# Expert tiles of 256 rows, four to a unit, in nine groups of images instead of six

## The chip, the cores and the metric

The kernel runs on one core of one Trainium2 chip. The metric is the device time of one execution in microseconds (us), lower is better; an execution's time is that of its slowest core, and here there is one.

## The reference

The input is 32 images of 32 x 32 pixels with 128 channels, in fp32. Three layers follow one another, each with a residual:

```python
x = x + window_attention(group_norm(x))      # 8x8 windows, shifted by 4, 8 heads of 16, cosine attention with a bias
t = tokens(x)                                # 1024 tokens to an image
t = t + banded_attention(layer_norm(t))      # windows of 128 tokens, 4 heads of 32, each sees 32 tokens back
t = t + experts(layer_norm(t))

def experts(x):                              # 8 experts, hidden size 256
    probs = softmax(x @ gate_w + gate_b)
    top2_vals, top2_idx = top_k(probs, 2)    # two experts to a token
    for e in range(8):
        h = gelu(x @ W1[e] + b1[e])
        out += weight_of_e[:, None] * (h @ W2[e] + b2[e])
```

The change is in the third layer, whose work depends on the data: each token goes to two of eight experts.

## The kernel before, in words

**Passes.** `hybrid_kernel` runs a software pipeline over images: 36 passes i from -1 to 34 (`PASSES` is 35), each of eight steps t. In pass i the image i+1 is loaded and normalised, image i goes through window attention, the scores of i-1 and i-2 through banded attention (12 steps behind, `LAG`), and image i-3 is gated. Every engine has one hand-written list of instructions in that order, and they meet only at semaphores. In each step TensorE (PE) makes scores, VectorE (DVE) adds bias or mask and takes the row maximum, GpSimd (POOL) subtracts it (`below_max`), ScalarE (ACT) takes the exponential, PE transposes and multiplies by the values.

**Sorting by expert.** In pass d+3 the gate of image d computes for each token its two experts, weights, and places in a sorted buffer in DRAM (`gate_*`, L1453 to L1530). GpSimd then writes the image's rows there with 16 indirect DMAs (`scatter`, L1218; three steps of pass d+3 and the first of the next). Images are taken in groups (`GROUPS`, L32): a group has one sorted buffer `x_sorted` with a region for each of the eight experts. At the last image of a group DVE makes a table (`tile_table`, L1532): the buffer row and the expert of each tile of 512 rows. Since the numbers are known only on the chip, as many tiles are computed as the worst case needs, 2 x images x 1024 / 512 + 7.

**Units.** A tile of 512 rows with its expert's weights (a row of 642 floats on each of 128 partitions: W1, W2, both biases) is a unit, two units a pair. A pair needs: loading (`load_pair`, L455, on SyncE's queue SP; in the tail on ScalarE's), eight transposes (`slots_in`, L814), a copy of 1024 columns (`slots_copy`, L1072), four matmuls of 512 columns (`hidden`, L821), four gelus (`gelu`, L1079), sixteen matmuls of 128 columns in two halves each (`expert_out`, L829), two additions of b2 (`slots_back`, L1572) and two stores into `y_sorted` (`store_pair`, L501). Loads read their row number and expert out of the table with `value_load`.

`plan` (L163) lays pairs into the passes: up to three to a pass, in slots 0, 1, 2, whose rows are transposed in step t = 1, 3, 6 (`stage`, L416). The first pair of a group stands in slot 1 or 2 of the fourth pass after the group's last image. Before it, `load_pair` waits for the table and for all scatters of the group, copies one tile of zeros behind each of the eight experts' rows (L462 to L469), waits until these have landed, and only then loads the first rows. What fits into no pass is left for the tail after the last pass.

**Gathering.** When a group's rows are stored, GpSimd reads them back for each image with 16 indirect DMAs (`gather`, L1227), and DVE weights, adds and stores (`sum_experts`, L1579). Passes take one image, from pass 29 (`TWO_SUMS_FROM`) two; what is left follows in the tail. From pass 32 on GpSimd puts a memset of a scratch tile after every indirect DMA (`apart`, L1239), but not behind the gathers of the last four images (`UNPAUSED`). In the tail DVE has the sum of an image behind every 2.5 pairs (L438 to L441):

```python
for c in range(first_tail_sum, IMAGES):
    at = max([at] + [n + 1 for n, u in enumerate(tail) if pairs[u].group == group_of[c]]) + PAIRS_PER_SUM
    (tail_sums[int(at)] if at < len(tail) else late_sums).append(c)
```

While there are no pairs (`i < first_slots`), PE runs one matmul of the identity by 512 columns in every step, whose result nobody reads (L867).

## Time and profile before

| | us |
|---|---|
| median of 3 runs | 3075.22 |
| the three runs | 3070.97, 3075.22, 3096.71 |
| span of the profiled execution, first to last instruction | 3088.7 |

The span is that of one more execution, under the profiler; what of it lies around the span the profile does not give. It is 13.5 us (0.4%) above the median. Times in the trace count from the start of the span. PE busy is matmul time, PEld the loading of its stationary operand; SPq and ACTq are DMAs issued by SyncE and ScalarE. A pass is recognised on PE by L801 (and L745), which stand in its step 4. The stretches of the rows below run from step 4 of one pass to step 4 of the next, or over several such.

### The profile page before, as it was taken

How to read it: one execution, taken by the hardware profiler on the slowest of the kernel's cores; microseconds unless marked ns; L12 is line 12 of the kernel's file. 1: busy time of each engine (PE TensorE's matmuls, PEld its weight loads, DVE VectorE, ACT ScalarE, POOL GpSimd, SP SyncE). 2: the span in 40 equal slices, each digit the busy share in tenths (PEclk: the TensorE clock that was granted, in tenths of full speed). 3: DMA queues.
4: the chain of work that ended last, by engine and by line, in shares of the span. 5: the costliest groups of instructions: out<-in, count | busy, mean ns of one | idle time of the engine just before them, and what ended most of it. 6: DMA issues, size and time to landing. Idle time of an engine off the chain costs nothing.

```text
span 3088.7 us, 77036 instructions
## 1 busy us (share of the span) xinstructions
PE 2544.2 (82%) x27338; PEld 1794.8 (58%) x27338; DVE 1965.5 (64%) x5091; ACT 1865.7 (60%) x3409; POOL 1914.2 (62%) x2270
## 2 busy tenths in 40 slices
PE   6898889989888899889988988899888887676830
PEld 3565655556666666666666666666665665554520
DVE  4577777777666666777676676767776765522222
ACT  3666656666767677677776677767777654432310
POOL 1335555555444444576666576666667878779986
PEclk9998888888999999899999999999999988788965
DMA  5223333334445454144333343434343434456743
GB/s 208 104 110 117 117 132 150 147 127 138 147 173 182 161 183 161 60 148 123 100 122 117 107 144 122 126 96 127 119 149 111 131 109 135 123 171 203 244 127 91
DMA packets 262427, 421.99 MB, mean 137 GB/s; under 512 B 41740, under 2 KB 141080, under 8 KB 261280
## 3 DMA queue, kind: packets, MB, share of 16 engines
q1 hardware_dynamic: 219232, 327.69, 31.2%
q0 software_dynamic: 32768, 67.17, 7.7%
q10 hardware_dynamic: 10048, 22.19, 2.2%
q8 instruction: 223, 3.65, 0.5%
q14 instruction: 156, 1.28, 0.1%
HBM read 198.26 MB, written 231.22 MB: 139 GB/s over the span
## 4 chain that ended last, share of the span: by engine, by line
PE 48%; POOL 17%; ACT 15%; issue 10%; DVE 7%; DMA 2%; ACTq 1%; SPq 1%; POOLq 0%; DVEq 0%
PE bank_m L834 7%; POOL yg L1233 7%; PE bank_m L827 4%; PE bank_to L761 4%; POOL x_sorted L1223 4%; PE bank_s L801 4%; PE bank_s L807 3%; PE bank_s L716 3%; ACT pt_sb_a L1051 2%; POOL xin L1243 2%; PE bank_to L770 2%; PE bank_s L729 2%; ACT L1178 2%; ACT v_a L1036 2%; PE bank_s L739 2%
## 5 line engine op out<-in xcount | busy, mean ns | idle before, releaser
L1223 POOL DMA_INDIRECT x_sorted<-xn_c,place_i x512 | 534.3, 1044 | 282.1 <-PE bank_s L700 109.2
L1233 POOL DMA_INDIRECT yg<-y_sorted,place_i x512 | 521.4, 1018 | 241.1 <-PE bank_to L783 107.5
L1216 POOL TENSOR_TENSOR s_sb_a<-s_sb_a,mx_a 128x512 f32<-128x512 f32 x256 | 267.8, 1046 | 587.7 <-DVE mx_a L1607 586.9
L1599 DVE TENSOR_TENSOR s_sb_a<-bank_s,bias_a 128x512 f32<-128x512 f32 x256 | 176.6, 690 | 355.3 <-PE bank_s L700 257.7
L827 PE MATMUL bank_m<-xe,wk_e 128*128 128x512 f32 x552 | 280.5, 634 | 37.7 <-ACT hid L1084 27.7
L834 PE MATMUL bank_m<-wk_e,hid 128*128 128x128 f32 x2208 | 283.3, 291 | 0.9 <-ACT hid L1084 0.9
L834 PEld LDWEIGHTS bank_m<-wk_e,hid 128*128 128x128 f32 x2208 | 277.7, 208 | 2.2 <-issue 1.9
L1216 POOL TENSOR_TENSOR s_sb_b<-s_sb_b,mx_b 128x512 f32<-128x512 f32 x256 | 269.7, 1054 | 11.5 <-DVE mx_b L1607 11.5
L761 PE MATMUL bank_to<-k_consts,p_sb_b 128*128 128x128 f32 x1024 | 179.0, 300 | 92.2 <-ACT pt_sb_a L1051 56.1
L1051 ACT ACTIVATE pt_sb_b<-bank_to 128x512 f32<-128x512 f32 x256 | 152.5, 596 | 146.4 <-PE bank_to L761 145.7
L1207 POOL TENSOR_TENSOR km_a<-qk_a,k_consts 128x128 f32<-128x128 f32 x512 | 215.7, 445 | 40.0 <-DVE qk_a L1451 35.4
L1056 ACT ACTIVATE p_sb_a<-s_sb_a 128x512 f32<-128x512 f32 x256 | 160.7, 628 | 122.1 <-POOL s_sb_a L1216 121.6
L1084 ACT ACTIVATE hid<-bank_m,wk_e 128x512 f32<-128x512 f32 x276 | 184.2, 686 | 78.7 <-PE bank_m L827 71.4
L700 PE MATMUL bank_s<-km_a,qk_a 32*64 32x128 f32 x4096 | 123.8, 296 | 112.9 <-POOL km_a L1207 52.3
L1056 ACT ACTIVATE p_sb_b<-s_sb_b 128x512 f32<-128x512 f32 x256 | 161.3, 630 | 72.1 <-POOL s_sb_b L1216 69.9
L827 PEld LDWEIGHTS bank_m<-xe,wk_e 128*128 128x128 f32 x552 | 98.5, 199 | 174.3 <-issue 134.9
L761 PEld LDWEIGHTS bank_to<-k_consts,p_sb_b 128*128 128x128 f32 x1024 | 113.5, 147 | 136.8 <-ACT pt_sb_a L1051 98.6
L761 PE MATMUL bank_to<-k_consts,p_sb_a 128*128 128x128 f32 x1024 | 167.3, 286 | 26.0 <-ACT p_sb_a L1056 25.8
L1068 ACT ACTIVATE sum_inv<-bank_to 128x256 f32<-128x256 f32 (+1 forms) x268 | 99.7, 372 | 139.8 <-PE bank_to L783 120.6
L1602 DVE TENSOR_TENSOR s_sb_b<-bank_s,k_consts 128x512 f32<-128x512 f32 x256 | 174.0, 680 | 13.7 <-ACT p_sb_b L1056 11.8
L1584 DVE TENSOR_TENSOR yg<-yg,weight 128x2048 f32<-128x2048 f32 x32 | 74.8, 2338 | 161.0 <-DMA yg<-y_sorted,place_i 161.0
L1576 DVE TENSOR_TENSOR yo<-bank_m,wk_e 128x512 f32<-128x512 f32 x138 | 94.9, 689 | 126.2 <-PE bank_m L834 106.8
(221 smaller groups left out, 6266.7 us busy)
## 6 DMA issues: line engine op xcount, KB each, us to landing
y_sorted<-t_back SPq DMA_DIRECT2D x192, 512.0 KB, 5.5
y_sorted<-yo SPq DMA_DIRECT2D x170, 256.0 KB
wk_e<-in_w_experts_dram SPq DMA_DIRECT2D x134, 321.0 KB
xs<-x_sorted SPq DMA_DIRECT2D x134, 256.0 KB
t_kept<-t SPq DMA_DIRECT2D x64, 256.0 KB
t_back<-t_kept SPq DMA_DIRECT2D x32, 512.0 KB
xin<-in_x_dram SPq DMA_DIRECT2D x128, 112.0 KB
x_res<-in_x_dram SPq DMA_DIRECT2D x256, 56.0 KB
```

The lines of the kernel that those rows point to most:

```text
L761: last = tr(T[:, P * j:P * j + P], p_sb[w][:, j, :], ident)
L827: mm(banks[:, ch, :], w[:, P * ch:P * ch + P], xe[:, m, :], start=True, stop=True).then_inc(z_ready, 1)
L834: last = mm(banks[:, m, P * j:P * j + P], hid[:, CH * m + ch, P * j:P * j + P], w[:, HID + P * ch:HID + P * ch + P], start=(ch == 0), stop ...
L1051: func(flat(pt_sb[w][:, :, :]), T, ACT.Copy).then_inc(pt_copied[w], 1)
L1056: func(flat(p_sb[w][:, :, :]), flat(s_sb[w][:, :, :]), ACT.Exp, scale=1.0 if w == 0 else float(DB) ** -0.5).then_inc(p_ready[w], 1)
L1084: func(hid[:, CH * m + ch, :], banks[:, ch, :], ACT.Gelu, bias=w[:, B1_AT + ch:B1_AT + ch + 1]).then_inc(gelu_ready, 1)
L1207: op = pool.tensor_tensor(km_a[:, n % 2, h, :], keys, const("pair_mask")[:, h:h + 1].to_broadcast([P, P]), ALU.mult)
L1216: pool.tensor_tensor(s[:, :, :], s[:, :, :], m[:, :, None].to_broadcast(shape), ALU.subtract).then_inc(s_sub[w], 1)
L1223: pool.indirect_dma_start(out=x_sorted[group_of[d] % XSIDES].ap(), out_offset=bass.IndirectOffsetOnAxis(ap=place_i[:, d, n:n + 1], axis=0) ...
L1233: pool.indirect_dma_start(out=yg[:, c % 2, n, :], out_offset=None, in_=y_sorted[side].ap(), in_offset=bass.IndirectOffsetOnAxis(ap=place_i ...
L1599: tt(s_sb[0][:, :, :].rearrange("p (r h) n -> p r (h n)", h=2), scores, bias_a[:, kind, :, :].rearrange("p (r h) n -> p r (h n)", h=2), AL ...
L1602: tt(s_sb[1][:, :, :], scores, const("mask_b")[:, None, :].to_broadcast([P, HB, P]), ALU.add).then_inc(s_added[1], 1)
```

## The change

- A tile has 256 rows (`SLOTS`), and a unit is two tiles (`PART = 2`) that each have their own row number, expert and weights. A unit has 512 rows as before, and its buffers are `ROOM` = 512 columns of rows and two sets of weights. A group's worst case falls from 2 x images x 2 + 7 tiles of 512 rows to 2 x images x 4 + 8 tiles of 256.
- Loads and stores are issued by tile: 8 loads to a pair instead of 4, 4 stores instead of 2. A matmul of `hidden` and a gelu take 256 columns and are twice as many.
- `GROUPS` is (3,4,4,4,4,4,4,3,2). The sorted buffers shrink from 65536 to 36864 rows, so filling `y_sorted` takes 108 DMAs instead of 192, clearing the spare rows of `x_sorted` 6 instead of 12.
- `TWO_SUMS_FROM` is 24.
- To make room, weights and places are kept for 16 images, some small tiles share one buffer, and constants that only the start needs lie in a buffer of the gather.

What `plan` makes of these numbers:

| | before | after |
|---|---|---|
| units, pairs | 170, 88 | 164, 82 |
| pairs in passes, in the tail | 68, 20 | 69, 13 |
| first pass with pairs | 10 | 6 |
| passes where a group's first pair is loaded (slot) | 10, 17, 23 (1), 28 (2), 33 (1), tail | 6, 10, 14, 18, 22, 26, 30 (1), 33 (2), tail |
| stretches from step 4 of pass i with fewer than 3 pairs, first pair to pass 29 | 15, 22, 28 (2.5), 16 (0) | 8 (2), 9 (0), 13, 17, 21, 25, 29 (1) |
| images summed in passes, in the tail | 20, 12 | 23, 9 |
| passes that sum two images | 29 to 32 | 24, 26, 27, 30, 31 |
| tail: after which pair (from 0) the sums stand that come before the last pair | 2, 5, 7, 10, 12, 15, 17 | 2, 5, 7, 10, 12 |

```diff
-GROUPS = (7, 7, 6, 5, 4, 3)
-SLOTS = 512
+GROUPS = (3, 4, 4, 4, 4, 4, 4, 3, 2)
+SLOTS = 256
 SUB = SLOTS // P
+PART = 2
+ROOM = PART * SLOTS
+KEPT = 16
...
-MAX_TILES = TOP * MOST // SLOTS + E - 1
+MAX_TILES = TOP * MOST // SLOTS + E
...
-TWO_SUMS_FROM = 29
+TWO_SUMS_FROM = 24
...
-        tiles = list(range(TOP * size * TOKENS // SLOTS + E - 1))
+        tiles = list(range(0, TOP * size * TOKENS // SLOTS + E, PART))
...
-                row = eng.value_load(tiles[0:1, kth:kth + 1], min_val=0, max_val=BUFFER - SLOTS)
-                expert = eng.value_load(tiles[0:1, MAX_TILES + kth:MAX_TILES + kth + 1], min_val=0, max_val=E - 1)
-                rows = x_sorted[side].ap()[bass.ds(row, SLOTS), :].rearrange("(p j) d -> p (j d)", p=P)
-                eng.dma_start(xs_b[b], rows).then_inc(tile_in[b], 16)
-                weights = w_experts[bass.ds(expert, 1), :, :].rearrange("e p n -> (e p) n")
-                eng.dma_start(wk_b[b], weights).then_inc(tile_in[b], 16)
+                for h in range(PART):
+                    at = kth + h
+                    row = eng.value_load(tiles[0:1, at:at + 1], min_val=0, max_val=BUFFER - SLOTS)
+                    expert = eng.value_load(tiles[0:1, MAX_TILES + at:MAX_TILES + at + 1], min_val=0, max_val=E - 1)
+                    rows = x_sorted[side].ap()[bass.ds(row, SLOTS), :].rearrange("(p j) d -> p (j d)", p=P)
+                    eng.dma_start(xs_b[b][:, SLOTS * h:SLOTS * h + SLOTS], rows).then_inc(tile_in[b], 16)
+                    weights = w_experts[bass.ds(expert, 1), :, :].rearrange("e p n -> (e p) n")
+                    eng.dma_start(wk_b[b][:, h, :], weights).then_inc(tile_in[b], 16)
...
-                pe.wait_ge(tile_in[b], 32 * use)
+                pe.wait_ge(tile_in[b], 32 * PART * use)
...
-                    mm(banks[:, ch, :], w[:, P * ch:P * ch + P], xe[:, m, :], start=True, stop=True).then_inc(z_ready, 1)
+                    for h in range(PART):
+                        own = slice(SLOTS * h, SLOTS * h + SLOTS)
+                        last = mm(banks[:, ch, own], w[:, h, P * ch:P * ch + P], xe[:, m, own], start=True, stop=True)
+                    last.then_inc(z_ready, 1)
...
-                    func(hid[:, CH * m + ch, :], banks[:, ch, :], ACT.Gelu,
-                         bias=w[:, B1_AT + ch:B1_AT + ch + 1]).then_inc(gelu_ready, 1)
+                    for h in range(PART):
+                        own = slice(SLOTS * h, SLOTS * h + SLOTS)
+                        last = func(hid[:, CH * m + ch, own], banks[:, ch, own], ACT.Gelu,
+                                    bias=w[:, h, B1_AT + ch:B1_AT + ch + 1])
+                    last.then_inc(gelu_ready, 1)
```

Two places show how instructions move. First ScalarE in the tail, kernel before: the load of the second unit of a pair (it stands twice in a row, once to a unit; `xs` is the rows, `wk_e` the weights, TENSOR_LOAD and ISA are `value_load` and address arithmetic), then the gelus of the pair before it and the copy of the next.

```order
L476 TENSOR_LOAD table
L476 ISA x2
L477 TENSOR_LOAD table
L477 ISA x2
L479 ISA
L479 DMA xs<-x_sorted 128x512
L481 ISA
L481 DMA wk_e<-in_w_experts_dram 128x642
L1084 ACTIVATE hid<-bank_m,qk_a 128x512 x2
L1084 ACTIVATE hid<-bank_m,wk_e 128x512 x2
L1077 ACTIVATE xe<-bank_s 128x1024
```

The same place after the change:

```order
L482 TENSOR_LOAD table
L482 ISA x2
L483 TENSOR_LOAD table
L483 ISA x2
L485 ISA
L485 DMA xs<-x_sorted 128x256
L487 ISA
L487 DMA wk_e<-in_w_experts_dram 128x642
L1097 ACTIVATE hid<-bank_s,wk_e 128x256 x8
L1088 ACTIVATE xe<-bank_to 128x1024
```

The load now stands four times in a row ahead of the gelus, each with half the rows and the whole weights, and there are eight gelus of half the width.

Second, SyncE in pass 33, kernel before: behind the store of slot 0's pair comes the load of slot 2's.

```order
L513 DMA y_sorted<-yo 128x512
L476 TENSOR_LOAD table
L476 ISA x2
L477 TENSOR_LOAD table
L477 ISA x2
L479 ISA
L479 DMA xs<-x_sorted 128x512
```

After the change, the same place (the store is the last of four):

```order
L520 DMA y_sorted<-yo 128x256
L469 TENSOR_LOAD table
L469 ISA x2
L472 ISA
L472 DMA x_sorted<-x_sorted 16x2048
L469 TENSOR_LOAD table
```

The eight copies of zeros of a new group now stand here between the store and the load; in the kernel before, pass 33 has them in slot 1, ahead of this store.

## Rows read from the trace of the kernel before

**Rows 1.** Chain of waits, from 2734.1 to the end: its summary line.

```profile
by line: POOL yg L1233 41.1%; issue 15.6%; POOL xin L1243 13.8%; DMA qk_a<-in_w_experts_dram 3.6%; DMA wk_e<-in_w_experts_dram 3.3%; POOL x_sorted L1223 3.0%; PE bank_m L827 1.8%; PE bank_s L834 1.5%; DMA yg<-y_sorted,place_i 1.5%; DVE yg L
```

**Rows 2.** Timeline, DVE: start, length, line, form, count, idle before and releaser.

```profile
2793.31 2.29 DVE L1584 TENSOR_TENSOR yg<-yg,weight 128x2048 f32<-128x2048 f32 x1 [20.97 <-DMA yg<-y_sorted,place_i]
...
2993.66 2.29 DVE L1584 TENSOR_TENSOR yg<-yg,weight 128x2048 f32<-128x2048 f32 x1 [15.90 <-DMA yg<-y_sorted,place_i]
...
3078.93 2.29 DVE L1584 TENSOR_TENSOR yg<-yg,weight 128x2048 f32<-128x2048 f32 x1 [16.17 <-DMA yg<-y_sorted,place_i]
```

**Rows 3.** GpSimd by line, 2765 to 3062.5: duration min/median/max in ns.

```profile
L1233 POOL DMA_INDIRECT yg<-y_sorted,place_i x180: 940/951/2736, 2765.8 to 3061.4; - x180
L1243 POOL MEMSET xin<- x129: 538/539/551, 2765.1 to 2992.1; 128x512 f32 x129
```

**Rows 4.** Windows: length, busy PE PEld DVE ACT POOL (instructions), PE clock, DMA share, GB/s.

```profile
751.10:1175.70 424.60, 381.26 (x4326) 276.27 (x4327) 271.40 (x765) 305.53 (x546) 193.44 (x240) 0.96 0.48 167
1328.90:1761.20 432.30, 388.81 (x4326) 282.17 (x4326) 295.66 (x780) 305.73 (x546) 274.03 (x321) 0.94 0.38 117
1839.90:2264.00 424.10, 380.23 (x4319) 276.03 (x4319) 298.81 (x794) 304.64 (x545) 272.88 (x319) 0.96 0.38 115
1255.00:1328.90 73.90, 62.29 (x741) 43.14 (x739) 59.81 (x162) 47.21 (x94) 54.10 (x64) 0.89 0.36 108
1175.70:1255.00 79.30, 69.15 (x826) 51.70 (x826) 53.56 (x152) 55.41 (x103) 37.44 (x46) 0.93 0.39 138
...
2346.10:2438.40 92.30, 79.47 (x874) 57.30 (x869) 67.81 (x159) 61.41 (x110) 77.32 (x80) 0.93 0.42 126
2438.40:2535.90 97.50, 82.05 (x851) 58.39 (x847) 64.70 (x146) 60.24 (x106) 77.53 (x80) 0.88 0.39 119
2535.90:2625.70 89.80, 65.15 (x655) 48.00 (x654) 55.37 (x143) 43.52 (x79) 77.59 (x89) 0.89 0.40 122
2625.70:2706.20 80.50, 55.98 (x406) 41.40 (x405) 42.74 (x98) 34.60 (x64) 57.29 (x71) 0.77 0.41 126
...
2734.10:3088.70 354.60, 171.76 (x921) 118.36 (x921) 86.89 (x96) 71.02 (x96) 296.56 (x355) 0.75 0.55 169
```

**Rows 5.** Windows, steps 4 of passes 6 to 30 in one.

```profile
461.90:2438.40 1976.50, 1763.94 (x20039) 1265.17 (x20038) 1389.46 (x3737) 1376.71 (x2511) 1186.87 (x1395) 0.94 0.41 134
```

**Rows 6.** Timeline, SP and PE, first pair of a group in pass 17.

```profile
1300.49 9.75 SPq L468 DMA_DIRECT2D x_sorted<-x_sorted  x8
1314.38 0.37 SPq L479 DMA_DIRECT2D xs<-x_sorted  x1
...
1317.16 0.33 SPq L481 DMA_DIRECT2D wk_e<-in_w_experts_dram  x1
...
1321.40 0.66 PE L818 MATMUL bank_m<-k_consts,xs 128*128 128x128 f32 x4 [0.56 <-DMA wk_e<-in_w_experts_dram]
```

**Rows 7.** Timeline, pass 33: DVE and PE around slot 2.

```profile
2698.59 0.68 DVE L1576 TENSOR_TENSOR yo<-bank_m,wk_e 128x512 f32<-128x512 f32 x1
...
2712.51 1.06 PE L818 MATMUL bank_m<-k_consts,xs 128*128 128x128 f32 x8 [1.07 <-DVE yo L1576]
```

**Rows 8.** ScalarE by line and form: count, busy us, mean ns, idle before.

```profile
L1084 ACT ACTIVATE hid<-bank_m,wk_e 128x512 f32<-128x512 f32 x276 | 184.2, 686 | 78.7 <-PE bank_m L827 71.4
...
L1051 ACT ACTIVATE pt_sb_b<-bank_to 128x512 f32<-128x512 f32 x256 | 152.5, 596 | 146.4 <-PE bank_to L761 145.7
...
L1068 ACT ACTIVATE sum_inv<-bank_to 128x256 f32<-128x256 f32 x244 | 93.4, 383 | 137.6 <-PE bank_to L783 120.6 <-PE bank_to L773 12.7 <-issue 1.1
```

**Rows 9.** Timeline, ScalarE in the tail: a pair's loads, and the new group's.

```profile
2759.31 0.34 ACTq L479 DMA_DIRECT2D qk_a<-x_sorted  x1
...
2761.49 0.34 ACTq L479 DMA_DIRECT2D qk_a<-x_sorted  x1
...
2838.98 9.54 ACTq L468 DMA_DIRECT2D x_sorted<-x_sorted  x8
2853.14 0.35 ACTq L479 DMA_DIRECT2D qk_a<-x_sorted  x1
```

More of the change, by code:

```diff
@@ L79, in _columns @@
     at = 0
-    for name, width in (("identity", P), ("group_mean", P), ("head_ones", P), ("pair_mask", 2), ("earlier", P),
-                        ("tri", E * E), ("mask_a", 4 * WTOK), ("mask_b", P), ("ones_a", DB), ("ones_b", DB),
+    for name, width in (("identity", P), ("group_mean", P), ("head_ones", P), ("pair_mask", 2),
+                        ("tri", E * E), ("mask_b", P), ("ones_a", DB), ("ones_b", DB),
                         ("thresholds", THRESHOLDS), ("tile_index", MAX_TILES), ("tile_rows", MAX_TILES),
@@ L89 @@
 CONST_WIDTH = _columns()
+EARLIER_AT, MASK_A_AT, EARLY_WIDTH = 0, P, P + 4 * WTOK
 def shape_constants():
     c = np.zeros((P, CONST_WIDTH), np.float32)
+    early = np.zeros((P, EARLY_WIDTH), np.float32)
     def put(name, value):
@@ L108, in shape_constants @@
     put("pair_mask", ch[:, None] // DA % 2 == np.arange(2)[None])
-    put("earlier", ch[:, None] < ch[None])
+    early[:, EARLIER_AT:EARLIER_AT + P] = ch[:, None] < ch[None]
     put("ones_a", ch[:, None] // WTOK == np.arange(DB)[None] // DA)
@@ L288, in hybrid_kernel @@
-        weight = sb("weight", [P, IMAGES, TOP * TILES])
+        place_i = sb("place_i", [P, KEPT, TOP * TILES], U32)
+        weight = sb("weight", [P, KEPT, TOP * TILES])
         seen = sb("seen", [1, E])
-        over = sb("over", [1, E, THRESHOLDS])
+        over = cmp_flat[0][0:1, 0:E * THRESHOLDS].rearrange("p (e n) -> p e n", e=E)
         need_tiles = sb("need_tiles", [1, E])
-        below = sb("below", [1, E, E])
+        below = cmp_flat[0][0:1, E * THRESHOLDS:E * (THRESHOLDS + E)].rearrange("p (e f) -> p e f", e=E)
@@ L310, in hybrid_kernel @@
-        yo = sb("yo", [P, 2, SUB, D])
+        xs_b = [sb(f"xs{n}", [P, ROOM])[:, :] for n in range(4)]
+        wk_b = [sb(f"wk_e{n}", [P, PART, PACK_W])[:, :, :] for n in range(4)]
+        xs_b += [flat[:, 0:ROOM] for flat in qk_flat]
+        wk_b += [flat[:, ROOM:ROOM + PART * PACK_W].rearrange("p (n w) -> p n w", n=PART) for flat in qk_flat]
+        xe = sb("xe", [P, 2, ROOM])
+        hid = sb("hid", [P, 4, ROOM])
+        yo = sb("yo", [P, 2, PART * SUB, D])
         yg = sb("yg", [P, 2, TOP * TILES, D])
@@ L815, in slots_in @@
                 b, use = buffer_of(q)
-                pe.wait_ge(tile_in[b], 32 * use)
-                for j in range(SUB):
+                pe.wait_ge(tile_in[b], 32 * PART * use)
+                for j in range(PART * SUB):
                     last = tr(dst[:, P * j:P * j + P], xs_b[b][:, P * j:P * j + P], ident)
@@ L831, in expert_out @@
                 pe.wait_ge(gelu_ready, CH * end)
-                for j in range(SUB):
+                for j in range(PART * SUB):
                     for ch in range(CH):
                         last = mm(banks[:, m, P * j:P * j + P], hid[:, CH * m + ch, P * j:P * j + P],
-                                  w[:, HID + P * ch:HID + P * ch + P], start=(ch == 0), stop=(ch == CH - 1))
+                                  w[:, j // SUB, HID + P * ch:HID + P * ch + P], start=(ch == 0), stop=(ch == CH - 1))
                 last.then_inc(y_done, 1)
@@ L1583, in sum_experts @@
                     dve.wait_ge(gathered[c % 2], 16 * TOP * TILES * (c // 2 + 1))
-                    tt(rows, rows, weight[:, c, :, None].to_broadcast([P, TOP * TILES, D]), ALU.mult).then_inc(summed, 1)
+                    tt(rows, rows, weight[:, c % KEPT, :, None].to_broadcast([P, TOP * TILES, D]), ALU.mult).then_inc(summed, 1)
                 if 1 in steps:
```

76 lines of the change are left out of this document (35 added, 41 removed).

## The prediction

> **What bounds the kernel now.** I read the windows first, then the chain of waits, then the timeline at the places that the diff touches. The windows of three passes with three pairs each last 424.6, 432.3 and 424.1 us [rows 4], 15 stretches in 1281.0 us, so 85.4 each; PE is busy for 90% of that at a granted clock of 0.94 to 0.96, nearly always on its upper level of 2.4 GHz. These passes are PE's. The stretch without a pair lasts 73.9 us and the one with 2.5 pairs 79.3: a pair costs about 4 us of a pass, not the 8 to 10 that it keeps PE busy, since it fills gaps. Where GpSimd sums two images beside three pairs the stretch grows to 92.3 and 97.5 us, POOL busy for 77 of them. In the tail GpSimd is the bound: 296.56 us busy in 354.6, PE half idle [rows 4], and the chain gives 41.1% to the gathers and 13.8% to the memsets behind them [rows 1]. So the tail is counted in images to sum, the passes in pairs and in stalls of PE.
>
> **(a) Fewer images in the tail.** Twelve are summed there now, nine after. The rate is read off DVE's first instruction of a sum: seven sums from 2793.31 to 2993.66, 28.6 us each, then four from there to 3078.93, 21.3 us each [rows 2]. The difference is the memsets: an indirect DMA takes 951 ns and a memset 539 [rows 3], sixteen of each and about 0.16 us between them make 26.4, and two long gathers at an image's start the rest. The last four stay without memsets, so the three that leave are of the slow sort: 3 x 28.6 = **-86 us**.
>
> **(b) ScalarE's pace there.** It issues the tail's loads, 2.18 us to one [rows 9]. A pair goes from two loads to four (the first order listings), each with a DMA of rows and one of weights: 4.4 to 8.7 us. A pair's cycle (copy, loads, gelus, the wait in between) is now about 10 us and becomes 14; 2.5 pairs then take 35 us, more than the 28.6 of a sum, so GpSimd would now wait for pairs in the tail's middle. The tail has only 13 pairs, and one group (two images) starts in it, with 9.54 us of zeros and 4.6 us until the next load [rows 9]. Thirteen pairs of 14 us are 182, with zeros and first load of the last group 196; GpSimd has gathered the seven images ahead of that group after 5 x 28.6 + 2 x 21.3 = 186: **+10**, between 0 (the gathers of passed groups fill in) and 30.
>
> **(c) The last passes.** Passes 32 and 33 sum none; now 32 sums two, with 32 x 1.65 = 53 us of GpSimd over two stretches. Their POOL load falls from 77.59 and 57.29 us [rows 4] to about 51 and 31, and PE with 65.15 and 55.98 becomes the bound. I put 89.8 at 76 (a stretch with a pair or two) and 80.5 at 61 (PE's time and 5): **-33**, between -15 and -45. But the group that starts in slot 2 of pass 33 has its zeros behind the store of the pair before (the second order listings). DVE finishes what is stored at 2698.59, and PE needs the new rows at 2712.51 [rows 7]. Behind 2698.59 now stand four stores of about 1.1 us, the zeros (9.75), 4.1 to the first load [rows 6], three loads more and their landing of 4.2 (1317.16 to 1321.40): 4.6 + 9.8 + 3.9 + 7.3 + 4.3 = 30, with the wake-up 32. It ends near 2731, 18 us late: **+18**, between 5 (if what stands ahead of it comes earlier too) and 28.
>
> **(d) The loop.** From pass 6 to 30 it takes 1976.5 us now [rows 5], among it four passes without pairs at the start. After, pairs run from pass 6 on: 17 stretches with three pairs, one of two (78), one of none (73.9), five of one (76, between 73.9 and 79.3) [rows 4]: 17 x 85.4 + 78 + 73.9 + 380 = 1983.7. Summing two images in 24, 26 and 27 adds 7 where both halves of the stretch have it (92.3 - 85.4) and 2 in four others; another table costs DVE 2. 1983.7 + 17 - 1976.5 = **+24**, between 10 and 40.
>
> **(e) Starts of groups.** Seven now stand in slot 1 of a pass of the loop. In pass 17 the first rows are issued at 1314.38, the last weights at 1317.16, 2.8 us later, and PE starts at 1321.40 after 0.56 us of wait [rows 6]: there is no slack left. With four tiles the last weights come about 3 x 2.18 + 0.4 = 7 us behind the first rows, 4 us later than now. What is queued behind PE's wait is the whole pass, as PE is its bound. I take 3.6 a start, **+25**; the ends are 1 and 7 each, 7 to 49.
>
> By the Trainium skill, DMA: Bandwidth & Descriptors, section "Anatomy of one DMA", a transfer costs about 2.0 us fixed plus its bytes at some 436 GB/s, 2.75 us for the 329 kB of weights. The trace has 4.2 us from issue to PE's start. By the page each start would be some 1.5 us shorter, the sum 10 us lower; the trace's number is used.
>
> **(f) Gelus of half the width.** A gelu of 512 columns takes 686 ns; an ACTIVATE of 256 takes 383 and one of 512 596 on the same engine [rows 8], so about 170 ns are fixed. Two halves cost 2 x (0.383 + 0.09/2) to 2 x 0.47, 0.08 to 0.25 us more than one. Four a pair: 0.3 to 1 us for ScalarE, which is busy for 305 of 425 us. PE waits for it once a pair, so I let 0.2 through: 82 x 0.2 = **+15**, between 0 and 41. PE's columns are the same; its shortest matmuls, of 128 columns, take 1.06 / 8 = 0.13 us [rows 7], so what is fixed in one is less than that, four more to a pair at half of it are 21 us at most, and I add none.
>
> **Priced at nothing.** SP issues 8 loads and 4 stores to a pair instead of 4 and 2: some 7 us a pair more of a queue that mostly waits for DVE; the cover is that a pair's loads go out 12 to 20 us ahead of PE. If that cover went, a pair would cost what a start does, 4 us. The extra weights (0.66 MB a pair) raise a DMA share of 0.38 to 0.48 [rows 4] to about 0.45 to 0.55. Passes with fills in them (424.6 for five) are no longer than those without, so fewer fills give nothing: 0, with -5 as the other end.
>
> **The sum.** -86 + 10 - 33 + 18 + 24 + 25 + 15 = -27 us against the profiled span of 3088.7: 3061.7. The median is 0.9956 of that span, so the changed kernel comes to **3048 us**, 0.9% less.
>
> **Rivals.** *B, the stalls stay hidden.* The passes' other work has enough slack that starts, narrow gelus and slot 2 of pass 33 cost a third: 25 + 15 + 18 become 19, and (b) 0. The sum is -86 - 33 + 24 + 19 = -76, 3000 us. For it: pairs already fill PE's gaps at half their price. Against it: PE waits at L818 with the present loads [rows 6].
>
> *C, sparse passes lose the clock (slower).* Six stretches with one or two pairs spread over the loop, and the filler matmul runs only before the first pair. The last passes, similarly thin, were granted 0.77 (between the levels of 1.2 and 2.4 GHz, so almost half of the time on the lower), against 0.94 [rows 4]. With 0.77 in place of 0.9 a stretch with 60 us of matmuls is 10 us longer: +60, 3108. It decides once a sparse stretch falls below about 0.85. Against it: the stretch without any pair got 0.89 and took 73.9.
> The Trainium skill, TensorE: Matmul & The Clock Gate, section "Loop structure matters more than you think", says that matmuls between waits for DMA run cold. That speaks for C, whose stalls at L818 are such waits; the granted clock of pass 17, 0.94 with its wait, speaks against.
>
> *D, ScalarE sets the tail.* If four loads and narrow gelus make a pair's cycle 18 us rather than 14, 13 pairs and the group's start need about 260 us and the four last sums stand behind them: +40, 3088. It decides from 16 us on. For it: each load holds register reads that no activation may pass. Against: now 10 us with 4.4 of loads.
>
> *E, gathers in passes cost what they save.* The 48 gathers moved into passes at 1.27 us (0.951 and the gap to the next) are 61 us of GpSimd; if they all lengthen the passes, as 97.5 against 85.4 suggests for two in one, the loop costs 46 us more, 3094. Against: one image to a pass costs nothing visible, and only three passes of the loop take two.
>
> **Chances.** Forecast 0.42 (its own range 3025 to 3080), B 0.27, C 0.12, D 0.11, E 0.08. A measurement tells about 1% of this kernel from no change: below 3044.5 is faster, above 3106 slower. Forecast: 0.43 of it faster, 0.05 slower. B: nearly all faster. C: half slower; D and E: a third slower each, as several terms may add up with theirs. Together 0.45 faster, 0.40 same, 0.15 slower. The range is 2998 to 3108: from B's time to C's.
>
> **What would show it.** After: DVE has nine sums in the tail at 28.6 and 21.3 us (a), wider where GpSimd waits for pairs (b, D, read on the gap between DMAs of rows on ScalarE's queue). PE waits 3 to 5 us on the weights' DMA at the first transposes of each group (e), and near 18 us in slot 2 of pass 33 (c); waits below 1 us there mean B. Stretches from step 4 to step 4: 85.4 with three pairs, 76 with one (d), with the granted clock beside them for C. A gelu of 256 below 0.43 us clears (f). Two things would make the forecast wrong outright: three-pair passes that are longer than 87 us, as SP's issue or DMA traffic is then no cover, and a pass from 6 to 10 that waits for GpSimd, where scatter, gather and pairs meet earlier than now.

## Result and profile after

| | before | after |
|---|---|---|
| median (runs shared on one chip), us | 3081.51 | 3122.41 (3117.60 to 3126.44) |
| ratio, 95% interval | | 1.012 (1.0082 to 1.0158) |
| span of the profiled execution, us | 3088.7 | 3115.7 |

The change makes the kernel 1.2% slower. The forecast was 0.9% faster, 3048 us, and its range ended at 3108. Of the two profiled executions the second is 27.0 us longer, where the sum gave 27 us shorter; the medians lie 41 us apart, as the profiled execution is the shortest of the changed kernel's four. The kernel before scatters too: of the 72 executions that ran beside the experiments 16 took 3065 to 3076 us at a mean granted clock of 0.916 to 0.921 and 56 took 3080 to 3102 at 0.903 to 0.913, and its profiled one, at 0.907, is of the longer kind.

Cut at the same step 4 of the passes as in [rows 4, 5], the difference is:

| part of the span | before | after | difference | forecast |
|---|---|---|---|---|
| up to step 4 of pass 6 | 461.7 | 463.2 | +1.5 | 0 |
| loop, passes 6 to 30 | 1976.7 | 2059.9 | +83.2 | (d)+(e)+(f) = +64 |
| passes 30 to 34 | 295.8 | 292.0 | -3.7 | (c) = -33 + 18 = -15 |
| tail | 354.6 | 300.6 | -54.0 | (a)+(b) = -86 + 10 = -76 |

The last three parts came out worse than forecast, by 19, 11 and 22 us, and none of their signs was wrong. The first part hides larger differences: the stretches 3 and 4, with the same instructions, are 10 us shorter at a higher clock (0.97 instead of 0.88), the one ahead of step 4 of pass 0 is 7 us longer, and the one before step 4 of pass 6, with the first pairs and a group's start (one of the seven of (e), so 3.6 of the 64 belong here), is 6 us longer. A stretch is named here by the pass in whose step 4 it begins.

The windows of the changed kernel (length, busy PE PEld DVE ACT POOL with instructions, granted clock, DMA share, GB/s): two stretches with three pairs, a sparse one with a group's start, one with two sums, the loop, three of the last passes, the tail.

```profile
1472.61:1562.99 90.38, 81.23 (x896) 64.49 (x892) 59.17 (x156) 62.79 (x122) 54.18 (x65) 0.91 0.47 136
...
795.64:881.77 86.13, 76.82 (x896) 60.36 (x892) 59.20 (x156) 62.79 (x122) 54.09 (x64) 0.96 0.47 137
1740.49:1819.94 79.45, 64.39 (x784) 47.59 (x780) 63.75 (x166) 50.06 (x100) 57.39 (x66) 0.91 0.39 112
1996.52:2092.15 95.63, 80.77 (x896) 63.46 (x892) 67.92 (x159) 63.09 (x122) 57.41 (x64) 0.89 0.44 124
463.24:2523.12 2059.88, 1797.50 (x20560) 1395.80 (x20555) 1442.12 (x3785) 1417.62 (x2751) 1265.04 (x1472) 0.92 0.45 131
2621.36:2701.95 80.59, 64.13 (x678) 52.36 (x677) 50.26 (x129) 45.09 (x91) 49.40 (x55) 0.92 0.50 142
2701.95:2769.07 67.12, 52.52 (x452) 43.46 (x451) 34.87 (x107) 37.78 (x78) 31.35 (x39) 0.90 0.41 124
2769.07:2815.13 46.06, 21.33 (x143) 18.42 (x142) 12.84 (x40) 12.47 (x22) 24.08 (x32) 0.72 0.40 121
2815.13:3115.70 300.57, 135.62 (x737) 116.06 (x737) 65.50 (x75) 55.71 (x117) 212.48 (x256) 0.72 0.58 171
```

Look at the first two rows beside [rows 4]. They do the same work (896 matmuls), but one takes 90.38 us and the other 86.13. The idle time of PE is the same in both, 9.2 and 9.3 us (length less busy); what differs is how long the matmuls last, 81.2 against 76.8, and the granted clock, 0.91 against 0.96: a larger part of the stretch at 1.2 instead of 2.4 GHz. Twelve such stretches with one sum or none have a mean of 88.0 us at a clock of 0.936; before it was 85.2 at 0.960 over thirteen. With the few of each kernel that these means leave out it is 87.8 at 0.939 over thirteen and 85.4 at 0.957 over fifteen.

The wait at a group's first transposes, the end of one row's answer (line 826: what PE waited for before it, us and times), and slot 2 of pass 33 in the timeline:

```profile
  DMA wk_e<-in_w_experts_dram: 31.0, 8
```

```profile
2765.97 9.82 SPq L472 DMA_DIRECT2D x_sorted<-x_sorted  x8
2778.85 0.37 SPq L485 DMA_DIRECT2D xs<-x_sorted  x1
...
2786.23 0.33 SPq L487 DMA_DIRECT2D wk_e<-in_w_experts_dram  x1
```

```profile
2785.30 1.08 PE L826 MATMUL bank_m<-k_consts,xs 128*128 128x128 f32 x4 [10.95 <-DMA wk_e<-in_w_experts_dram]
2790.41 1.12 PE L826 MATMUL bank_m<-k_consts,xs 128*128 128x128 f32 x4 [4.03 <-DMA wk_e<-in_w_experts_dram]
```

Of the 31.0 us, 15.0 are pass 33: the zeros, 3.1 us until the first rows, four loads and their landing stand ahead of PE there, as (c) said. The other six waits share 16 us on PE itself, and its weight loads wait at the same place besides.

The sums in the tail, on DVE, where [rows 2] had one every 28.6 and then every 21.3 us:

```profile
2874.95 2.29 DVE L1598 TENSOR_TENSOR yg<-yg,weight 128x2048 f32<-128x2048 f32 x1 [5.79 <-DMA yg<-y_sorted,place_i]
2914.74 2.28 DVE L1598 TENSOR_TENSOR yg<-yg,weight 128x2048 f32<-128x2048 f32 x1
2957.43 2.28 DVE L1598 TENSOR_TENSOR yg<-yg,weight 128x2048 f32<-128x2048 f32 x1
3003.47 2.28 DVE L1598 TENSOR_TENSOR yg<-yg,weight 128x2048 f32<-128x2048 f32 x1
...
3105.90 2.29 DVE L1598 TENSOR_TENSOR yg<-yg,weight 128x2048 f32<-128x2048 f32 x1 [16.18 <-DMA yg<-y_sorted,place_i]
```

The first gaps are 39.8, 42.7 and 46.0 us, and no DMA of a gather is what three of these sums waited for: in DVE's list a sum stands behind 2.5 pairs, and the pairs come late. From the first sum to the last are 231 us; at GpSimd's own pace it would be 4 x 28.6 + 4 x 21.3 = 200. ScalarE in the tail shows why (one pair's cycle; x4 are a unit's four gelus):

```profile
2847.88 1.02 ACT L1088 ACTIVATE xe<-bank_s 128x1024 f32<-128x1024 f32 x1 [0.74 <-issue]
2849.19 0.34 ACTq L485 DMA_DIRECT2D qk_a<-x_sorted  x1
2849.70 1.64 ACTq L487 DMA_DIRECT2D qk_a<-in_w_experts_dram  x1
...
2858.14 0.34 ACTq L487 DMA_DIRECT2D qk_a<-in_w_experts_dram  x1
2858.58 1.57 ACT L1097 ACTIVATE hid<-bank_s,wk_e 128x256 f32<-128x256 f32 x4 [9.68 <-issue]
2861.71 0.84 ACT L1097 ACTIVATE hid<-bank_s,wk_e 128x256 f32<-128x256 f32 x2 [1.56 <-PE bank_s L837]
...
2864.94 1.02 ACT L1088 ACTIVATE xe<-bank_to 128x1024 f32<-128x1024 f32 x1 [0.74 <-issue]
```

From copy to copy are 17.1 us, 9.7 of them between the copy and the first gelu, in which ScalarE only issues loads; behind it come waits of 1.56 and 0.81 us for PE's matmuls and 0.74 before the copy. The mean of the five cycles from 2832.36 to 2910.28 is 15.6.

### The profile page after: what moved, and what is told of

It reads as the page before. It is cut to its first block, busy times and chain, and to the rows that moved or that the text cites. A ratio compares the mean times of both kernels' runs of the same rounds, so it can differ in the third digit from the quotient of the medians.

```text
span 3115.7 us, 81145 instructions
## 1 busy us (share of the span) xinstructions
PE 2535.4 (81%) x27786; PEld 1935.3 (62%) x27786; DVE 1986.8 (64%) x5127; ACT 1903.1 (61%) x3721; POOL 1855.8 (60%) x2190
## 4 chain that ended last, share of the span: by engine, by line
PE 46%; ACT 15%; issue 11%; POOL 11%; DVE 6%; SPq 5%; DMA 3%; ACTq 3%; POOLq 0%; DVEq 0%
PE bank_m L845 8%; PE bank_m L837 5%; PE bank_to L769 4%; POOL x_sorted L1237 4%; PE bank_s L809 3%; POOL yg L1247 3%; PE bank_s L815 3%; PE bank_s L724 3%; PE bank_s L737 2%; ACT pt_sb_a L1062 2%; ACT L1192 2%; PE bank_to L778 2%; PE bank_m L826 2%; ACT hid L1097 2%; ACT v_a L1047 2%
## 5 line engine op out<-in xcount | busy, mean ns | idle before, releaser
L1237 POOL DMA_INDIRECT x_sorted<-xn_c,place_i x512 | 528.0, 1031 | 306.2 <-PE bank_s L708 99.1
L1247 POOL DMA_INDIRECT yg<-y_sorted,place_i x512 | 505.1, 987 | 311.3 <-PE bank_to L791 124.7
L837 PE MATMUL bank_m<-xe,wk_e 128*128 128x256 f32 x1136 | 296.0, 407 | 58.0 <-ACT hid L1097 48.0
L845 PE MATMUL bank_m<-wk_e,hid 128*128 128x128 f32 x2272 | 301.9, 298 | 1.0 <-ACT hid L1097 1.0
L845 PEld LDWEIGHTS bank_m<-wk_e,hid 128*128 128x128 f32 x2272 | 297.5, 215 | 1.6 <-issue 1.6
L837 PEld LDWEIGHTS bank_m<-xe,wk_e 128*128 128x128 f32 x1136 | 217.6, 202 | 121.5 <-issue 74.2
L1097 ACT ACTIVATE hid<-bank_m,wk_e 128x256 f32<-128x256 f32 x568 | 229.1, 475 | 77.8 <-PE bank_m L837 60.4
L1221 POOL TENSOR_TENSOR km_a<-qk_a,k_consts 128x128 f32<-128x128 f32 x512 | 224.4, 461 | 44.3 <-DVE qk_a L1464 39.8
L1062 ACT ACTIVATE pt_sb_a<-bank_to 128x512 f32<-128x512 f32 x256 | 149.3, 583 | 48.2 <-PE bank_to L769 48.0
```

The costliest lines, as they stand in the source:

```text
L837: last = mm(banks[:, ch, own], w[:, h, P * ch:P * ch + P], xe[:, m, own], start=True, stop=True)
L845: last = mm(banks[:, m, P * j:P * j + P], hid[:, CH * m + ch, P * j:P * j + P], w[:, j // SUB, HID + P * ch:HID + P * ch + P], start=(ch = ...
L1062: func(flat(pt_sb[w][:, :, :]), T, ACT.Copy).then_inc(pt_copied[w], 1)
L1097: last = func(hid[:, CH * m + ch, own], banks[:, ch, own], ACT.Gelu, bias=w[:, h, B1_AT + ch:B1_AT + ch + 1])
L1221: op = pool.tensor_tensor(km_a[:, n % 2, h, :], keys, const("pair_mask")[:, h:h + 1].to_broadcast([P, P]), ALU.mult)
L1237: pool.indirect_dma_start(out=x_sorted[group_of[d] % XSIDES].ap(), out_offset=bass.IndirectOffsetOnAxis(ap=place_i[:, d % KEPT, n:n + 1], ...
```

## The experiments

The experiments ran in four sets (four kernels, four, three, one), each beside its own runs of the kernel before, whose median was 3083 to 3094 us; the changed kernel itself did not run again, so it is compared through the ratios to before. The ratios with their intervals are as recorded and differ from the quotients of the medians by up to 0.3%. Each kernel was profiled once, and the tables of stretches are of that execution. *Theory 1* in the expectations is that halved gelus make PE wait a little longer on each pair, and that these small waits cost it granted clock as well.

### Gelus of half the width, alone

```diff
-                    func(hid[:, CH * m + ch, :], banks[:, ch, :], ACT.Gelu,
-                         bias=w[:, B1_AT + ch:B1_AT + ch + 1]).then_inc(gelu_ready, 1)
+                    for h in range(2):
+                        own = slice(256 * h, 256 * h + 256)
+                        last = func(hid[:, CH * m + ch, own], banks[:, ch, own], ACT.Gelu,
+                                    bias=w[:, B1_AT + ch:B1_AT + ch + 1])
+                    last.then_inc(gelu_ready, 1)
```

> The kernel before, with each gelu of 512 columns issued as two of 256; nothing else differs, the output is the same. Theory 1 (narrow gelus make PE wait a little longer on each pair, and these small waits make it lose granted clock as well): the stretches with three pairs of the loop go from 85.4 us to about 88, as they are after the change, and the granted clock there from 0.957 to about 0.93; 17 stretches x 2.5 and a few in the tail are +40 to +50 us, a time near 3125 us. Rival (the longer stretches come from the doubled loads and stores, not from the gelus): only the ScalarE time that I priced at 0.2 us a pair, +15 us or less, 3090 us, and a clock as before.

Measured: 3134.06 us against 3094.41 for before, ratio 1.010 (1.0053 to 1.0148). In the profile the loop takes 2036.6 us instead of 1976.7, the tail 354.6 as before. The windows of this kernel:

```profile
1526.90:1615.60 88.70, 79.65 (x874) 58.39 (x870) 59.12 (x156) 62.79 (x123) 54.26 (x65) 0.92 0.36 113
...
462.90:2499.50 2036.60, 1812.92 (x20045) 1312.57 (x20040) 1389.14 (x3737) 1406.96 (x2736) 1173.99 (x1395) 0.92 0.40 130
```

and of two neighbouring stretches of the kernel before:

```profile
1501.67:1585.26 83.59, 75.17 (x873) 54.30 (x868) 59.17 (x156) 61.13 (x110) 55.05 (x65) 0.98 0.38 119
1585.26:1672.31 87.05, 77.87 (x873) 56.60 (x868) 59.08 (x156) 61.13 (x110) 54.77 (x65) 0.94 0.38 116
```

ScalarE is busy for 1.7 us more in a stretch (62.79 against 61.13), PE idle for 0.6 more on average (9.2 against 8.6), and the matmuls, the same ones, last 79.4 us instead of 76.6, nearly five times what the idle time grew by. Before, stretches at 0.98 alternate with some at 0.92 to 0.94; with halved gelus nearly all lie at 0.92. In PE's waits over the loop, the one on the gelus is small in both (before first, then halved; us, times, longest):

```profile
PE bank_m L827 <- ACT hid L1084: 24.7, 52, 0.6
```

```profile
PE bank_m L827 <- ACT hid L1086: 33.1, 54, 0.7
```

8.4 us more, less than the 15 of (f). In all, PE's idle time in the loop grows by 11 us and its busy time, for the same matmuls, by 49: that is the clock. The profiled execution is the longest of its four (3150.7 us; the others 3116.0 to 3144.9), so the size is better read from the times: 40 us between the medians, 31 by the ratio. The rival of this run (loads and stores) explains nothing of it, since neither was touched.

### Hidden matmuls of half the width, alone

The kernel before, with `hidden` issuing two matmuls of 256 columns for each of 512.

> The kernel before, with each hidden matmul of 512 columns issued as two of 256 with the same weights, gelus as wide as before. The prediction priced this at nothing (21 us at most). Expected: PE busy in the loop the same within 5 us, loop within 5 us of 1976.7 and the time the same as before. If the second weight load or the second issue costs PE 0.05 us each, 4 more to a pair are 14 us, and the granted clock falls as with the halved gelus.

Measured: 3090.24 against 3087.18 us, ratio 1.0019 (0.9983 to 1.0055); the loop 1966.7 us, three-pair stretches 85.5 at 0.957. Free, as priced; the loop's 10 us less lie in the pairless passes 6 to 8, at a clock of 0.95 instead of 0.88.

### The changed kernel with wide gelus

> The changed kernel with one gelu of 512 columns in place of two of 256; both tiles of a unit then get the first tile's b1, so what it leaves out is the second expert's bias of the hidden layer. Theory 1 (gelus and the clock): the stretches with three pairs fall from 88.0 to about 85.5 us, clock from 0.93 to 0.955, the loop is 40 us shorter, 3080 us in all. Rival (loads and stores): 10 us shorter at most, 3112 us, stretches of 87.5.

Measured: 3084.84 us, ratio to before 0.9969 (0.9952 to 0.9986). The loop takes 2024.2 us, 35.7 less than after the change; its one-sum three-pair stretches fall from 88.0 to 85.7, the clock from 0.936 to 0.955, PE's idle time from 9.3 to 8.6. The tail is 301.2, unchanged. By the profiles the gelus' width is worth 36 us here and 60 in the kernel before; by the times some 38 (medians) to 46 (ratios) here and 31 to 40 there.

### One weights load to a unit

> The changed kernel with one weights load a unit: both tiles use the first tile's weights and biases, so the second expert's weights are left out; 164 of 328 weights loads go, 54 MB. Theory 1: only the starts (PE's wait on the weights 3.9 us each, eight of them, to about 1.5: -20 us) and the tail (a pair's loads on ScalarE 8.7 us to about 7: cycle 15.6 to 14, -15 us) gain, the three-pair stretches stay at 88; 3088 us. Rival (traffic or SyncE's issue sets the stretches): they fall to 85.5 too, 40 us more, 3050 us.

Measured: 3082.82 us, ratio 0.9957 (0.9928 to 0.9987). The three-pair stretches stay at 87.7, so the extra 54 MB and SyncE's issue cost them nothing, and the rival falls. The tail is 283.1, 17 us shorter, as expected. The loop is 20 us shorter too, but only 12 of it lie in the six stretches of the loop with a start, where theory 1 put all 20: PE waits for no weights there, but it now waits for rows, 4.9 us over the loop where it had waited 11.1 for weights. The rest is scattered.

### The tail's loads on two queues

`load_pair` takes one unit: ScalarE issues the first of a pair, SyncE the second ahead of its stores.

```diff
             for n, u in enumerate(tail):
+                if n + 2 < len(tail):
+                    load_pair(sp, tail[n + 2], 1)
                 store_pair(u)
...
-                    load_pair(act, tail[n + 2])
+                    load_pair(act, tail[n + 2], 0)
```

> The changed kernel with the tail's loads shared: ScalarE issues those of a pair's first unit, SyncE those of its second. If ScalarE's issue sets the tail's pace (a pair every 15.6 us, an image's sum every 43 us), the pair falls to about 11 us, the sums come at GpSimd's own 28.6 us, and the tail loses 25 to 31 us: about 3093 us. If something else sets it (GpSimd, the last scatter, PE at its lower clock), the time stays within 8 us of 3122.

Measured: 3085.88 us, ratio 0.9979 (0.9956 to 1.0002). The tail takes 273.9 us, 27 less, within the expectation, and copies on ScalarE come every 10 us at first. The median is 37 us below the changed kernel's, 10 more than the tail gives and 7 below the expected 3093; the profile does not say where they are. But the sums come every 33 to 38 us and not every 28.6: the timeline of PE shows what took over.

```profile
2884.68 1.12 PE L828 MATMUL bank_s<-k_consts,xs 128*128 128x128 f32 x4 [16.72 <-DMA wk_e<-in_w_experts_dram]
```

```profile
2852.98 3.74 SPq L520 DMA_DIRECT2D y_sorted<-yo  x4
...
2873.63 3.48 SPq L544 DMA_DIRECT2D out_dram<-yg  x8
2878.68 0.37 SPq L485 DMA_DIRECT2D xs<-x_sorted  x1
```

SyncE's loads now stand behind the store of an image, which waits for its sum: nothing is issued between 2856.7 and 2873.2, and the load goes out at 2878.7. That queue is the next thing to mend.

### Hidden matmuls of the second unit moved behind other work

> The changed kernel, with PE's four hidden matmul pairs of a pair's second unit moved behind one piece of banded-attention work (1 to 1.9 us of matmuls) in two of three slots, so that the first unit's gelus have that time before PE wants their bank. Nothing else differs. The gelus stay narrow. If it is PE's wait on the narrow gelus (0.74 us a pair) that costs the granted clock, the wait goes in two pairs of three, the three-pair stretches fall from 88.0 towards 85 us at a clock of 0.95 or more, and the loop is 25 to 40 us shorter: about 3090 us against before at 3082. If it is ScalarE's longer gelu time as such, or the later gelus hold up what ScalarE does next, the stretches stay at 88 or grow, and the time stays at 3120 or above.

Measured: 3161.80 us, ratio 1.0247 (1.0186 to 1.0309): slower by another 1.3%, the opposite of what theory 1 expected. PE's waits over the loop, in the changed kernel and in this one:

```profile
PE bank_m L837 <- ACT hid L1097: 34.3, 56, 0.7
...
PE bank_to L769 <- ACT p_sb_a L1067: 18.2, 43, 0.6
```

```profile
PE bank_to L769 <- ACT p_sb_a L1073: 39.4, 62, 1.5
...
PE bank_s L737 <- DVE s_sb_a L1619: 29.4, 26, 2.9
```

The wait for gelus fell to 16 us, but ScalarE did the second unit's gelus later and with them the exponentials behind them, and PE waited for those: idle 10.0 us in a three-pair stretch instead of 9.3, clock 0.916, length 90.2. The run does not tell whether that one wait matters; it does show that moving a wait is not filling it, and again the clock is lower where PE idles more.

### Sums of two images from pass 29 only

`TWO_SUMS_FROM` is 29 again; the tail still has nine sums, as no group is stored earlier.

> The changed kernel with TWO_SUMS_FROM at 29, as before the change: passes 24 to 29 sum one image each, and the tail still gets nine, since only groups that are stored can be summed. The stretches 24, 26 and 27 (95.6, 94.0, 92.9 us) fall to the 88 of their neighbours, 28 may stay: 15 to 19 us shorter. If gathers cost a pass the same wherever they lie (the rival of the prediction that gives a gather back what it saves), the sums moved from 24, 26, 27 to 25, 28, 29 lengthen those instead, and the time is within 5 us of the changed kernel's.

Measured: 3097.89 us, ratio 1.0047 (1.0013 to 1.0081), 0.7% below the changed kernel's. The stretches 24, 26, 27 and 28 fall from 95.6, 94.0, 92.9 and 90.4 to 86.1, 86.1, 87.8 and 86.1; 25 and 29, which take a sum, rise by 3.7 and 2.4. The loop is 23.8 us shorter. Not all of that is the sums': 28 has a sum more than it had (POOL 54 us busy instead of 38) and is 4.3 us shorter all the same, at a higher clock with PE's idle time the same, 9.2 and 9.3. First 28 after the change, then 28 of this run:

```profile
2356.66:2447.05 90.39, 81.20 (x897) 64.50 (x892) 54.30 (x153) 62.79 (x122) 38.19 (x48) 0.91 0.35 101
...
2335.87:2421.94 86.07, 76.78 (x896) 60.17 (x892) 59.20 (x156) 62.74 (x122) 54.45 (x65) 0.96 0.45 131
```

The three second sums cost 22.6 us, and moving them cost 6.1 in 25 and 29: 16.5 for the schedule. They bought nothing: the tail is 298.8 us without them and 300.6 with them.

### Both of these

> The changed kernel with both the tail's loads on two queues and TWO_SUMS_FROM at 29. They touch different parts of the span, so the gains should add: 30 to 43 us from the tail and 15 from the loop, 1.5 to 1.9% below the changed kernel, faster than before by 0.3 to 0.7%.

Measured: 3073.40 us, ratio 0.9971 (0.9939 to 1.0003). Loop 2038.8, tail 270.5, each within 4 us of what the one edit alone gives, so in these parts the gains add. The time is 1.5% below the changed kernel's, at the lower end of the expectation and less than the 1.4% and 0.7% of the two edits alone: in this profile the part ahead of step 4 of pass 6 took 14 us more than after the change. The interval still touches no change.

### Work in PE's gaps

One more matmul of the identity in each of three steps, into the bank that the transposes behind it overwrite:

```diff
-            def transposed_probs(w, n):
+            def transposed_probs(w, n, busy=0):
+                if busy:
+                    mm(T[:, 0:busy], ident, k[:, 0:busy], start=True, stop=True)
                 pe.wait_ge(p_ready[w], n + 1)
...
-                    transposed_probs(1, nb - 1)
+                    transposed_probs(1, nb - 1, 256 if t in (1, 4) else 128 if t == 0 else 0)
```

> The kernel before with halved gelus, and on PE one matmul of the identity ahead of the transposes of the banded probabilities, where PE waits for ScalarE anyway: 256 columns (0.5 us) in steps 1 and 4, 128 in step 0, into a bank that the transposes overwrite. It adds 1.3 us of PE work to a pass, most of it in time that was idle (0.93, 0.93 and 0.38 us there). If PE's idle time near these places is what makes it lose the clock (theory 1 as it stands: 9.1 us idle and clock 0.92 in a three-pair stretch with halved gelus, 8.4 and 0.98 or 0.94 without), the clock in the three-pair stretches rises from 0.92 to 0.95 or more and the stretches fall from 88.7 to 84 to 86 us: the loop is 35 to 70 us shorter, about 3075 us. If the clock does not hang on these waits, the stretches stay at 88.7 or grow by up to 1 us.

> The changed kernel with the tail's loads on two queues, TWO_SUMS_FROM at 29, and the same three filler matmuls a pass. Against the version without them: if the filler gives back the clock, the three-pair stretches go from 87 to 84.5 us, 17 of them and some in the sparse ones, 40 us shorter, 3035 us. If it does not, the same time as without, 3073 us.

> The kernel before, gelus of 512 columns, with the same three filler matmuls a pass. Its three-pair stretches already have a granted clock of 0.98 in about half of them and 0.92 to 0.94 in the others (83.6 against 87 to 88.7 us). If the clock follows PE's idle time, the others rise to 0.98: stretches near 84, the stretches of the first ten passes (71.6 us at 0.88) shorten too, the loop 20 to 40 us shorter, about 3055 us. If the filler only repairs what the halved gelus broke, the time is that of before within 8 us.

Measured, ratio to before: with halved gelus 0.9996 (0.9972 to 1.0021), where without the filler it was 1.010; the changed kernel with two queues and sums 0.9882 (0.9847 to 0.9918) where it was 0.9971; the kernel before 0.9963 (0.9933 to 0.9993). A stretch and the loop of the first of them:

```profile
1480.20:1566.00 85.80, 76.29 (x877) 55.56 (x873) 59.04 (x156) 62.72 (x122) 54.18 (x65) 0.98 0.37 116
450.90:2435.70 1984.80, 1758.09 (x20187) 1270.17 (x20184) 1389.87 (x3737) 1407.29 (x2735) 1174.82 (x1395) 0.96 0.41 134
```

The means over the three-pair stretches with one sum or none (10 to 14, 17 to 20 and 23 to 26 where pairs are laid as before; 7, 10 to 12, 14 to 16, 18 to 20, 22 and 23 as after):

| | length | PE busy | idle | clock |
|---|---|---|---|---|
| before | 85.2 | 76.6 | 8.6 | 0.960 |
| before, filled | 85.8 | 77.4 | 8.4 | 0.958 |
| halved gelus | 88.6 | 79.4 | 9.2 | 0.922 |
| halved gelus, filled | 86.9 | 77.6 | 9.3 | 0.962 |
| changed | 88.0 | 78.8 | 9.3 | 0.936 |
| changed, wide gelus | 85.7 | 77.1 | 8.6 | 0.955 |
| changed, two queues and sums | 87.2 | 77.9 | 9.3 | 0.945 |
| the same, filled | 87.6 | 78.5 | 9.0 | 0.951 |

In the kernel with halved gelus more PE work makes the loop 52 us shorter: more matmuls were issued (20187 against 20045), yet PE was busy for 55 us less. Of the 52, 28 lie in the fifteen stretches with three pairs; there PE's idle time stayed at 9.2 to 9.3 us and the clock rose from 0.92 to 0.96. That shows that the halved gelus cost mainly by the clock, and that the clock is lost to what PE does around its waits. Another 18 lie in the stretches 6 to 9, which have no pairs but for the start of the first, so they are not the gelus'.

Two expectations missed. Before was to gain 20 to 40 us and gained 0.4%, nothing of it in the three-pair stretches. What it gained lies in the stretches 3 to 8, which have no pairs; before, then with the filler:

```profile
246.18:676.64 430.46, 385.44 (x4430) 259.33 (x4425) 326.68 (x882) 259.87 (x529) 239.72 (x289) 0.88 0.34 126
```

```profile
251.72:650.30 398.58, 346.05 (x4441) 234.92 (x4462) 330.85 (x882) 259.47 (x529) 238.81 (x289) 0.99 0.36 136
```

32 us less in six stretches, of which 12 are lost again in the stretches 10 to 29. And in the changed kernel, which has pairs from pass 6 on, the filler did not shorten the three-pair stretches; of the 9 us between the two profiles 20 were gained ahead of pass 6 and some lost behind, while the ratios differ by 0.9% and the medians by 0.6%. So the filler helps in the pairless passes wherever it was tried, and in the full ones only with halved gelus in the kernel before; why not in the changed kernel is open.

### Weights ahead of the wait for zeros

At a group's start the four weights loads are issued while the zeros land.

> The same with one more edit: at the start of a group the four weights loads are issued while the zeros land, and only the rows wait for the zeros. The last load is then issued 3.3 us behind the first rows instead of 7, and PE's wait for the weights at the first transposes (2 to 5 us in the sparse passes) should go to 0 or 1 us: seven starts, 15 to 25 us shorter than the version without. If the landing of the rows themselves is late, less than 5 us.

Measured: 3029.95 us, ratio to before 0.980 (0.9765 to 0.9836), 0.8% below the version without. PE's waits for DMA in the loop, without this edit and with it:

```profile
PE bank_m L830 <- DMA wk_e<-in_w_experts_dram: 15.9, 5, 4.4
```

```profile
PE bank_m L837 <- DMA xs<-x_sorted: 0.9, 2, 0.7
```

The seven stretches with a start are 4.5, 5.4, 6.5, 3.9, 4.1, 3.3 and 0.4 us shorter, 28 us, of which 19.5 are idle time of PE and 8.5 busy time. The first of them lies ahead of step 4 of pass 6, so 23.5 are the loop's, which is 25.7 shorter. The medians differ by 24.7 us, at the upper end of the expected 15 to 25. It is the fastest kernel of the study, ahead of before by 2.0% and of the changed one by about 3%.

## Why the prediction was wrong

The sum missed by 54 us between the two profiles: 22 in the tail, 19 in the loop, 11 in the last passes. Two steps made most of it. In (f) the mechanism failed: it priced a wait and left out the granted clock, 36 us for 15. In (b) ScalarE's pace was mis-sized and so was what it holds up, 32 us for 10. The forecast was moreover scaled from a median of three runs, 3075.22 us; that of the 72 later executions of the kernel before is 3091.0.

**(a) and (b), the tail.** The images that leave were rightly counted and priced; ScalarE's pace was not. I put a cycle at 14 us and the loss at 10; it is 15.6 and the loss 32 (354.6 - 86 = 268.6 against 300.6), just past the end of 30 that I gave. The loads were right (8.7 us issued, 9.7 seen until the first gelu). What I left out is that ScalarE's first gelu stands behind all the pair's loads in its list, so the gelus and their waits for PE, 1.56, 0.81 and 0.74 us, come wholly behind the loads and not beside. And I set the late pairs against GpSimd alone, while the sums stand in DVE's list behind a fixed number of pairs: each of the first sums slipped, not only the last group. This is the mechanism of rival D at 15.6 us instead of 18, just under the 16 from which it was to decide. Two queues gave back 27.

**(c), the last passes.** The stall in slot 2 of pass 33 was forecast at 18 us and its stretch grew by 18.1 (27.97 to 46.06). The relief was 33 in the forecast and is 22.5: 89.80 to 80.59 and 80.46 to 67.12. I had taken PE's time as the bound and PE still waits; these are 5 and 6 us in two stretches.

**(d), the loop's schedule.** Forecast 24, of which 15 for the sums of two images; undone, these gave 16.5, and 15.3 in the version with two queues. With 16.5 for the sums, 23.5 for the six starts in the loop and 36 for the gelus taken off, 7 of the loop's 83 us are left, where I had 9. So (d) held. That it comes out so closely is in part luck: between two profiles the passes 6 to 23 with the same instructions differ by 3 and by 7 us, and one stretch at another clock by 4.

**(e), the starts.** Forecast 25, 3.6 us a start; undone the seven gave 28. By the Trainium skill (DMA: Bandwidth & Descriptors, "Anatomy of one DMA": about 2.0 us fixed and the bytes at 436 GB/s) each start would have been 1.5 us shorter, 15 us for the seven; the page gives this for DMAs that GpSimd issues, and SyncE issues these. The runs stand with the trace's 4.2 us from issue to use.

**(f), narrow gelus: the step whose mechanism failed.** "I let 0.2 through: 82 x 0.2 = +15" counts ScalarE's time and PE's wait, and PE's wait for gelus did grow by only 8 to 10 us. The width measured 36 us in the changed kernel's profile (38 to 46 by the times) and 31 to 40 in the kernel before (60 in its profile), since PE lost granted clock as well, in stretches where it is the bound. ScalarE's own price was low too: a gelu of 256 takes 475 ns, so two cost 0.26 us more than one of 512, just past the end of 0.25 that I gave (and the formula beside the lower end, 0.08, gives 0.17; 82 x 0.2 is 16). I had asked about the clock only for sparse passes (rival C). Those with one pair had 0.89 to 0.91, above the 0.85 from which that rival decides; only the stretch without a pair fell below it, 0.83 and 81.4 us instead of 73.9. Most of the loss was in the full ones.

The Trainium skill describes the like in TensorE: Matmul & The Clock Gate, section "A second HAM failure mode: psum-queue depth-cycling": frequent short idles between groups of matmuls make the clock go back and forth. The trace agrees in kind: here some 19 idles of at most 1.0 us make 9 us in 88, and the clock falls one to three times in such a stretch, for 11.4 us on the mean against 6.8 before the change. The section that I cited instead, on loops that wait for DMA, was about gaps of another kind, and what I held against it was misread: the wait at L818 in pass 17 lies in the stretch at 0.89 [rows 4], not in those at 0.94.

**What stays open.** PE's idle time in a stretch orders most kernels of the table by clock, but not all: with the filler it is 9.3 us at 0.962. Within one kernel it orders nothing: before the change there are stretches with 8.2 to 8.4 us idle at 0.98, at 0.96 and at 0.92. So that more idle time means less clock is not shown; shown is that narrow gelus lower the clock and that matmuls in the gaps raise it. Which of the gaps decide was not found. Whether the tail, at 0.72 to 0.75, could be kept at the upper level was not tried.

## What to carry to other kernels

Price an instruction that is split, on an engine that another waits for, in two terms: the wait, and what the waiting TensorE loses in granted clock; here PE's busy time grew by 49 us and its idle time by 11 (profile of the kernel before with halved gelus). Compare stretches with the same work and look at busy time beside the clock before looking for a longer wait, and before reading 20 us off two profiles look at how far the executions of one kernel lie apart. When work leaves the tail's bound, find the engine that issues for it, with everything that stands in one list in front of the next result, since a list in fixed order turns one late pair into a late sum.

## What the runs showed that I had not expected

- A stretch with the same instructions lasts from 83.6 to 88.7 us in one execution of the kernel before, at clocks of 0.98 to 0.92, in steps: 83.6, 85.2, 87.0, 87.8, 88.7. PE's idle time differs by 1 us at most. It is 8.3 us in this one, as in the shortest:

```profile
2007.72:2095.54 87.82, 79.51 (x873) 58.26 (x869) 59.22 (x156) 61.13 (x110) 54.81 (x65) 0.92 0.37 114
```

- Passes 3 and 4 are the same instructions in all kernels here but those with the filler; they take 66.5 and 67.1 us at 0.97 in the changed kernel's profile and 72.1 and 71.6 at 0.88 in that of before and of four experiments. With the filler all four kernels have 66 to 67 us there. The kernel before with halved hidden matmuls was profiled at 3068.6 us and has 406.9 us in the stretches 3 to 8, where the profile of 3088.7 has 430.5: those six stretches alone can set two executions 20 us apart. Whether they do so in every execution no profile shows.
- For these matmuls fewer and wider gains nothing on PE: two matmuls of 256 columns cost what one of 512 does (ratio 1.0019, 0.9983 to 1.0055), while two gelus of 256 take 2 x 475 ns against 686.
